# A gated attention and expert kernel: expert outputs scattered to token rows, slot clears in small transfers, first tiles' rows loaded ahead

## The reference

```
x = x + tanh(g_xattn) * layernorm(residual_scale * (attention(layernorm(x), context, mask) @ Wo + bo))   # 16 heads of 16
y = layernorm(x)
logits = y @ w_router                      # 8 experts
top 2 of 8; softmax of the two             # weights of a token
h = relu(y @ w_fc[e])^2 ; out = h @ w_proj[e]      # for the two experts e of the token
x = x + tanh(g_ffn) * sum of the two outputs, weighted
```

## Time and profile before

| | |
|---|---|
| median of 3 executions | 1218.92 us (1215.73 to 1224.65) |
| the profiled execution: its own time | 1217.37 us |
| its span, first to last instruction | 1215.6 us |
| TensorE busy / weight loads | 1130.4 us (93%) / 1081.4 us (89%) |
| VectorE busy | 864.5 us (71%) |
| ScalarE busy | 660.6 us (54%) |
| GpSimd busy | 131.1 us (11%) |
| mean granted TensorE clock | 0.978 of full speed |

### The profile page before, as it was taken

One profiled execution on the slowest core, in us unless ns is written; L12 is line 12 of the kernel. 1 busy time (PEld: TensorE's weight loads), 2 busy tenths in 40 slices (PEclk: granted clock), 3 DMA queues, 4 the chain that ended last, 5 costly groups with the idle time before them and its releaser, 6 DMA issues.

```text
span 1215.6 us, 55794 instructions
## 1 busy us (share of the span) xinstructions
PE 1130.4 (93%) x24824; PEld 1081.4 (89%) x24824; DVE 864.5 (71%) x2001; ACT 660.6 (54%) x838; POOL 131.1 (11%) x144
## 2 busy tenths in 40 slices
PE   6899999999999999999999999999999999878891
PEld 6899899999999999999999999999999999867790
DVE  5667677777777677767777777767777767747766
ACT  4456565656565556656565656555565655443430
POOL 0000000010101001010101010100101010100036
PEclk9899999999999999999999999999999999989896
DMA  5132222213231323232321313132322232024214
GB/s 179 57 88 72 83 69 69 85 54 104 67 92 55 104 68 104 68 87 68 87 82 47 109 64 100 49 103 67 104 68 87 64 99 67 17 61 124 82 61 138
DMA packets 59486, 98.83 MB, mean 81 GB/s; under 512 B 13109, under 2 KB 41586, under 8 KB 59250
## 3 DMA queue, kind: packets, MB, share of 16 engines
q1 hardware_dynamic: 49730, 79.93, 21.7%
q10 hardware_dynamic: 6832, 8.92, 2.2%
q0 software_dynamic: 2688, 6.43, 1.7%
HBM read 70.17 MB, written 24.15 MB: 78 GB/s over the span
## 4 chain that ended last, share of the span: by engine, by line
PE 79%; DVE 10%; issue 4%; POOL 2%; DMA 2%; SPq 1%; ACT 1%; POOLq 0%; ACTq 0%; DVEq 0%
PE v_ps L563 21%; PE k_ps L566 20%; PE sc_ps L589 18%; PE o_ps L604 11%; DVE prob L1233 3%; POOL expert_out L488 2%; DVE kl L1014 2%; DVE vst L1029 1%; PE k_ps L621 1%; PE k_ps L628 1%; DVE c_lo L1020 1%; PE sc_ps L506 1%; DVE q_hi L1066 1%; PE sc_ps L507 1%; PE sc_ps L508 1%
## 5 line engine op out<-in xcount | busy, mean ns | idle before, releaser
L858 ACT ACTIVATE prob<-sc_ps,m_bias 125x896 f32<-125x896 f32 x384 | 377.1, 1008 | 354.1 <-PE sc_ps L589 353.6
L563 PE MATMUL v_ps<-wv_hi,c_hi 64*125 64x256 f32 x1520 | 311.9, 285 | 2.9 <-DVE c_lo L1020 2.6
L566 PE MATMUL k_ps<-c_hi,wk_hi 64*128 64x500 f32 x760 | 306.8, 404 | 0.0
L563 PE MATMUL v_ps<-wv_lo,c_hi 64*125 64x256 f32 x1520 | 302.1, 279 | 0.0
L563 PE MATMUL v_ps<-wv_hi,c_lo 64*125 64x256 f32 x1520 | 302.0, 278 | 0.0
L566 PE MATMUL k_ps<-c_lo,wk_hi 64*128 64x500 f32 x760 | 294.0, 387 | 0.0
L566 PE MATMUL k_ps<-c_hi,wk_lo 64*128 64x500 f32 x760 | 293.2, 386 | 0.0
L1029 DVE TENSOR_TENSOR vst<-v_ps,rowv 125x512 f32<-125x512 f32 x191 | 131.3, 687 | 185.4 <-PE v_ps L563 185.4
L1233 DVE TENSOR_SCALAR prob<-prob 125x896 f32<-125x896 f32 x384 | 233.1, 620 | 39.8 <-ACT prob L858 39.8
L589 PE MATMUL sc_ps<-q_lo,kh 64*125 64x224 f32 x1536 | 233.3, 272 | 12.9 <-issue 12.9
L563 PEld LDWEIGHTS v_ps<-wv_hi,c_hi 64*125 64x125 f32 x1520 | 226.8, 184 | 17.0 <-issue 5.9
(11 more groups left out here) (189 smaller groups left out, 1639.6 us busy)
## 6 DMA issues: line engine op xcount, KB each, us to landing
raw<-in_ctxT SPq DMA_DIRECT2D x96, 500.0 KB, 3.5
slot_rows<-zero_row SPq DMA_DIRECT2D x16, 896.0 KB, 8.8
w_raw<-in_we ACTq DMA_DIRECT2D x16, 256.0 KB, 8.0
rows<-slot_rows SPq DMA_DIRECT2D x32, 128.0 KB, 2.0
slot_out<-y SPq DMA_DIRECT2D x32, 128.0 KB, 1.9
rec<-inv_scratch SPq DMA_DIRECT2D x64, 56.0 KB, 2.0
xq<-in_x ACTq DMA_DIRECT2D x16, 112.0 KB, 3.7
xr<-in_x ACTq DMA_DIRECT2D x16, 112.0 KB, 4.5
```

Source lines behind the costliest of these rows:

```text
L563: v_last = pe.matmul(v_ps[0:TC, j * D:(j + 1) * D], c_s[v_rows, cs], w_m[v_rows, k, :], start=begin and j == 0, stop=end, skip_group_check ...
L566: k_last = pe.matmul(k_ps[:, half, 0:TG], w[k_rows, k, ws], c_m[k_rows, :], start=begin, stop=end)
L858: act.activation(prob[0:TC, c % PB, :].rearrange("p (c n) -> p c n", c=2), sc_ps[0:TC, 2 * (c % 2):2 * (c % 2) + 2, 0:NH * S // 2], ACT.Ex ...
```

## The change

- `slot_rows` gets 8 more columns (rows of 1056 bytes). Column 256 holds, as an integer, the row of a new DRAM tensor `expert_rows` (2 x 14 x 112 rows) to which the expert's output for this slot belongs: one row for each token and each of its two experts. Cleared rows carry a number past the end.
- `clear_slots(i, e)` clears 128 rows of one expert. There are 14 x 8 of them, one or two behind the load of each group; each waits until the one before it has landed. The very first waits for `dest_done`, set by VectorE in its preamble once the numbers are in place.
- `send(j, r)`: the first send of a pair (r = 0) stays where it was; VectorE then rewrites the number (`relabel`, u = 9), and the second (r = 1) goes out after `inv_std(2)`.
- Each tile's output is scattered to `expert_rows` by GpSimd (`send_back`) as soon as it is out of PSUM; numbers past the end are dropped. SP's stores and `rows_back` are gone.
- After the last scatter SP loads `expert_rows` in eight plain DMAs. Of each chunk of pairs VectorE combines all but the last pair; ScalarE scales and GpSimd adds that one. `out` is stored in five parts.
- The rows of the first tiles are loaded once k and v are computed and the sends have landed (seven tiles), and the others once the exponentials are done; `turn(0)` stands ahead of the last attention products.
- The table work is split over u = 7, 9 and 10 of the last pair, and the steps of `beside_experts` are moved.

The diff, cut to its core (declarations, and removed lines that the listing above shows, are left out):

```diff
+RR = 12
+RE = 7
+WR = D + 8
+SPARE = 2 * NS * PW
+CB = ((0, 4), (4, 8), (8, 12), (12, 14))
...
+            return {0: 0, 2: 3, 4: 6, 7: 12, 8: 14, 9: 15, 11: 18, 12: 20, 14: 23, 15: 24, 17: 26, 18: 28}[at]
...
+            def clear_slots(i, e):
+                if i == 0 and e == 0:
+                    sp.wait_ge(dest_done, 2)
+                wait(sp, zeroed, 16 * (i * NE + e))
+                sp.dma_start(slot_rows[e * CAP + i * P:e * CAP + (i + 1) * P, :], zero_row[:, :]).then_inc(zeroed, 16)
             def pair(i):
                 for q in range(PG):
...
                         gather_sums(i - 1)
                     if i > 0 or q >= 2:
                         load_group(i * PG + q, q % 2)
-                    if q == 2:
-                        clear_slots(i)
+                    if i < CAP // P:
+                        for e in ((0, 1), (2,), (3,), (4,), (5,), (6, 7))[q]:
+                            clear_slots(i, e)
                     if q == 4 and i > 0:
                         spread_inverses(i - 1)
                 if i > 0:
...
             def load_slots(u):
                 if u == 0:
                     sp.wait_ge(tab_done, 2)
-                    sp.wait_ge(zeroed, 16 * NP)
+                    sp.wait_ge(zeroed, 16 * NE * (CAP // P))
                     for r in range(2):
                         sp.wait_ge(sent[r], 16 * NS)
-                    sp.wait_ge(pv_done, B * NC)
-                wait(sp, turned, u - RR + 1)
+                    sp.wait_ge(kproj_done, KD * NP * PG)
+                    sp.wait_ge(vproj_done, 2 * NP * PG)
+                if u == RE:
+                    sp.wait_ge(exp_done, B * NC)
+                if u >= RR:
+                    sp.wait_ge(turned, u - RR + 1)
+                    sp.wait_ge(back[u % NB], 16 * ((u - RR) // NB + 1))
                 row = sp.value_load(tab[0:1, 1, u:u + 1], min_val=0, max_val=NE * CAP - SL)
...
+                sp.dma_start(rows[:, u % RR, :], slot_rows[bass.ds(row, SL), :]).then_inc(rows_in[u % RR], 16)
+            def load_outputs(b):
+                j0, j1 = CB[b]
+                for r in range(2):
+                    at = r * NS * PW
+                    sp.dma_start(expert_out[0:PW, r, j0:j1, :],
+                                 expert_rows[at + j0 * PW:at + j1 * PW, :].rearrange("(j p) d -> p j d", p=PW))\
+                        .then_inc(expert_in[b][r], 16)
             for u in range(RR):
                 load_slots(u)
             gather_sums(NP - 1)
             spread_inverses(NP - 1)
...
+            for u in range(RR, NU):
+                load_slots(u)
+                if u == RR + 3:
                     pack(NP - 1)
...
+            for u in range(NU - NB, NU):
+                sp.wait_ge(back[u % NB], 16 * (u // NB + 1))
+            for b in range(len(CB)):
+                load_outputs(b)
+            sp.wait_ge(acc_done, 2 * NE)
+            sp.dma_start(out[:, NS:NP, :], acc[0:PW, NS:NP, :]).then_inc(out_done, 16)
+            for b, (j0, j1) in enumerate(CB):
+                sp.wait_ge(sum_done[0], 2 * (j1 - 1 - b))
+                sp.wait_ge(sum_done[1], 2 * (b + 1))
+                sp.dma_start(out[:, j0:j1, :], acc[0:PW, j0:j1, :]).then_inc(out_done, 16)
+            sp.wait_ge(out_done, 16 * (len(CB) + 1))
...
+            def send(j, r):
+                if r == 0:
+                    pool.wait_ge(slot_done, j + 1)
+                    pool.wait_ge(zeroed, 16 * NE * min(j + 1, CAP // P))
+                else:
+                    pool.wait_ge(relabelled, j + 1)
+                wait(pool, sent[r], 16 * j)
+                pool.indirect_dma_start(slot_rows[:, :], bass.IndirectOffsetOnAxis(ap=slot_i[0:PW, j, r:r + 1], axis=0),
+                                        y_row[0:PW, j % 2, :], None).then_inc(sent[r], 16)
...
+                    send(j, 0)
                 if not first:
                     inv_std(2, i - 1)
+                for j in ranked(i):
+                    send(j, 1)
...
+            def send_back(u):
+                pool.wait_ge(y2_evac, u + 1)
+                wait(pool, back[u % NB], 16 * (u // NB))
+                pool.indirect_dma_start(expert_rows[:, :],
+                                        bass.IndirectOffsetOnAxis(ap=rows[:, u % RR, D:D + 1].bitcast(i32), axis=0),
+                                        y2[:, u % NB, :], None, bounds_check=SPARE - 1, oob_is_err=False)\
+                    .then_inc(back[u % NB], 16)
+            for u in range(NU):
+                send_back(u)
+                if u == 11:
+                    x_plus_beta(NP - 1)
+                    inv_std(1, NP - 1)
+                if u == 13:
+                    inv_std(2, NP - 1)
+            for b, (j0, j1) in enumerate(CB):
                 for r in range(2):
...
+                    pool.wait_ge(scaled, 2 * b + r + 1)
+                    wait(pool, sum_done[1], 2 * b + r)
+                    pool.tensor_tensor(acc[0:PW, j1 - 1, :], acc[0:PW, j1 - 1, :], expert_out[0:PW, r, j1 - 1, :], ALU.add)\
+                        .then_inc(sum_done[1], 1)
...
+            turn(0)
             for d in range(GC, 0, -1):
                 pv(NP - 1, PC - d)
-            turn(0)
...
+            act.wait_ge(weights_done, 1)
+            for b, (j0, j1) in enumerate(CB):
+                for r, weight in enumerate((pr1, pr2)):
+                    act.wait_ge(expert_in[b][r], 16)
+                    act.activation(expert_out[0:PW, r, j1 - 1, :], expert_out[0:PW, r, j1 - 1, :], ACT.Copy,
+                                   scale=weight[0:PW, j1 - 1:j1]).then_inc(scaled, 1)
...
+                if i < NS:
+                    dve.tensor_copy(label(i), dest_i[0:PW, i, 0:1])
+                normalised(2, i, y_row[:, i % 2, 0:D], acc[:, i, :]).then_inc(y_done, 1)
+            def label(i):
+                return y_row[0:PW, i % 2, D:D + 1].bitcast(i32)
+            def relabel(i):
+                for j in ranked(i):
+                    dve.wait_ge(sent[0], 16 * (j + 1))
+                    dve.tensor_copy(label(j), dest_i[0:PW, j, 1:2]).then_inc(relabelled, 1)
...
+                if u == 9 and final:
+                    tile_starts()
+                if u == 10 and final:
                     tile_table()
-                if u == 8 and final:
-                    rows_back()
+                if u == 9:
+                    relabel(i)
...
+            dve.wait_ge(ones_done, 5)
+            dve.tensor_copy(zero_row[:, D:D + 1].bitcast(i32), spare_c).then_inc(dest_done, 1)
+            dve.tensor_copy(dest_i[:, :, :], dest_c.rearrange("p (j r) -> p j r", r=2)).then_inc(dest_done, 1)
...
-                    wait(dve, y2_out[u % NB], 16 * (u // NB))
-                    dve.tensor_copy(y2[:, u % NB, :, :], sc_ps[:, 2 + u % 2, 0:SH * D].rearrange("p (h d) -> p h d", h=SH))\
-                        .then_inc(y2_evac, 1)
+                    wait(dve, back[u % NB], 16 * (u // NB))
+                    dve.tensor_copy(y2[:, u % NB, :], sc_ps[:, 2 + u % 2, 0:D]).then_inc(y2_evac, 1)
...
+            for b, (j0, j1) in enumerate(CB):
+                for r, weight in enumerate((pr1, pr2)):
+                    dve.wait_ge(expert_in[b][r], 16)
+                    if r == 1:
+                        dve.wait_ge(sum_done[0], 2 * (j0 - b) + j1 - 1 - j0)
+                    for j in range(j0, j1 - 1):
+                        dve.scalar_tensor_tensor(acc[0:PW, j, :], expert_out[0:PW, r, j, :], weight[0:PW, j:j + 1],
+                                                 acc[0:PW, j, :], ALU.mult, ALU.add).then_inc(sum_done[0], 1)
...
+    expert_rows = nc.dram_tensor("expert_rows", (SPARE, D), mybir.dt.float32, kind="Internal").ap()
```

More of the change, by code:

```diff
@@ L48 @@
 FILL = 10
[L51 removed]
+CST = (P, NE, HS, KD, KD, PW, NE, NE * NE, CAP // SL, NU, 1, 2 * NS)
 EPS = 1e-5
@@ L115, in gated_cross_attention_moe @@
         cst = sb("cst", [P, sum(CST)])
-        ident, rev_e, hmask, bk, bq, below_c, seg_c, upto_c, size_c, step_c = (cst[:, sum(CST[:i]):sum(CST[:i + 1])] for i in range(len(CST)))
+        ident, rev_e, hmask, bk, bq, below_c, seg_c, upto_c, size_c, step_c, spare_c, dest_c = (cst[:, sum(CST[:i]):sum(CST[:i + 1])] for i in range(len(CST)))
         rowv = sb("rowv", [P, 4 * D + 3])
@@ L435, in _ @@
             pool.memset(ones[:, :], 1.0).then_inc(ones_done, 1)
-            pool.wait_ge(ones_done, 4)
+            pool.memset(y_row[:, :, :], 0.0).then_inc(ones_done, 1)
+            pool.wait_ge(ones_done, 5)
             def inv_std(ln, i):
@@ L452, in expert_lo @@
                                    plain(we_hi[:, bass.ds(i, 1), :, :].squeeze(1)), ALU.subtract).then_inc(welo_done, 1)
-            def send(j):
-                pool.wait_ge(slot_done, j + 1)
-                pool.wait_ge(zeroed, 16 * (j + 1))
-                for r in range(2):
-                    wait(pool, sent[r], 16 * j)
-                    pool.indirect_dma_start(slot_rows[:, :], bass.IndirectOffsetOnAxis(ap=slot_i[0:PW, j, r:r + 1], axis=0),
```

(13 more changed lines are left out.)

98 lines of the change are left out of this document (20 added, 78 removed).

## The result

The changed kernel took 1269.06 us (median of 4 runs, 1266.10 to 1274.27) where the kernel before took 1219.6 on the same chip: a ratio of 1.0408, 95% interval 1.0356 to 1.0459. The sign was forecast; the size was not (1240, range 1210 to 1260). The profiled execution spans 1264.3 us, 48.7 more than before.

A forecast was written before the change was run, and what follows sets the result against it. TensorE, 79% of the chain, was taken to bound the kernel in the first 1070 us. Terms -16.5+7+36+12-6-1-10 = +21.5 on 1217.37 gave 1238.9, about 1240 for the median, range 1210 to 1260.

The forecast's parts named there:

- clears, the gaps: TensorE's 15 gaps, one per pair, 16.7 us in all, vanish with the 896 KB clears: -16.5 us.
- start: Three small clears ahead of context group 2's load delay the first exponential from 23.49 to 29.8: +7 us.
- second send: Pairs 3 to 14: y_rows waits for the later send, landing in 4.8 us; y transpose 3.0 us late: +36 us.
- clock: Behind that wait TensorE's clock drops, costing 1.7 us in 60% of twelve pairs: +12 us.
- last pair, experts: Split table work and earlier first expert rows give -6 us; scatters hidden in the expert stage and pack earlier give -1.
- tail: After the static experts, eight loads replace the gathers and VectorE does 20 multiply-adds instead of 28: -10 us.
- Rival 3: Worse contention at the second send: landing 6.0 us and a clock drop in all twelve pairs, 1263 us; chance 0.10.
- rival 4: Splitting the clears fails: fetches are delayed by anything queued, the 15 gaps stay, +16.5, 1256 us; chance 0.10.
- Rivals 1 and 2: Second send lands in 3.8 us, clock never falls, 1216 (chance 0.20); or lands in 2.5 us, 1200 (chance 0.13).

## Why the prediction was wrong

By its own steps, on the first kind of chip:

| step | predicted | measured | from |
|---|---|---|---|
| clears, the gaps | -16.5 | -21 | B 33.92 to 32.53, 15 times |
| start | +7 | +7.4 | first exponential |
| second send | +36 | +50.6 | A summed over 12 pairs, less 12 x 3.76 |
| clock | +12 | +25 | B over 32.53 (ten pairs, 20.4), the next two stretches over those with three buffers (4.8) |
| last pair, experts | -7 | -3 | +62.4 at the last pair's y transpose, +59.4 at the combine |
| tail | -10 | -10.7 | +59.4 to +48.7 |
| sum | +21.5 | +48 | span +48.7 |

The rows leave some 3 us between the first and the fifth term open: the split table work saved about 3 us ahead of the last pair's y transpose as well, which would make the clears some -19 and the fifth term some -5. The sum stays.

**The step that failed is the size of "The second send", the landing time of 4.8 us.** Its mechanism, place and count were right: buffer, parity, pairs 3 to 14, no slack at the y transpose. I took 4.8 as the mean of the first sends, which start beside a load (they took 4.0 to 6.0; my 3.8 for the fastest was a little low). The second send starts beside the same load and has w_raw and xr about it as well. I named these two and gave them no price. In the changed kernel the twelve landed in 5.4 to 7.2 us but for the control at 3.6, 6.3 in the mean, so even my upper bound of 6.0 was below most of them. The first sends, which now have small clears about them, took longer too, 5.6 in the mean. The two runs that took raw and then w_raw out of its way show what each was worth.

**The second failing size is the clock.** I took a drop of 3.4 us, as after the idle time in the earlier trace rows, in 60% of the pairs. The idle time was 4.5 us, the lower level lasted 6.8 us in nine pairs and 3.4 in two, about 5 of it behind the wait, and eleven of twelve pairs had it: 2 to 2.5 us for the 1.0 that I took in the mean. The two errors hang together: a landing 1.5 us later costs as much more wait, and the runs with waits of 4.5, 1.8 and 0.8 us had the drop in eleven, ten and none of twelve pairs. I had judged an idle time of 2.9 us to "lie at the edge" and taken a mean there; the load held back shows that already 1.8 us mostly brings the drop, so it was no edge, and the range should have held both sides in full. Rival 3, given 0.10, came nearest: 1263 from a landing of 6.0 and a drop in all twelve.

**What held.** The gaps went with the 896 KB transfers, so rival 4 fell; the small clears alone showed it in the kernel before. Rivals 1 and 2 fell with the landing time. The start was right to 0.4 us and was shown by undoing it. The tail was right: the 20 multiply-adds took 10.16 us for the 9.3 taken; that is read from the two profiles, and no run undid it. Of the last pair I had the order of events but somewhat too much gain: its y transpose now waits 3.24 us (0.30 before). That this and the two second sends in a row account for the rest is my reading; no run undid them either.

The Trainium skill's formula for such a send (DMA: Bandwidth & Descriptors, the anatomy of one DMA on the GpSimd path), 2.3 us here by my estimate, comes near the fastest of the 28 sends, 2.6, and is far below those that went beside loads (3.6 to 7.2).

## What to carry to other kernels

Before a send or a load is moved later, find the step that refills its buffer, and count buffers until that step waits for a transfer of the round before: here one more buffer turned +4.1% into -2.2%. Price a transfer by the company it will have at its new place, every queue counted, not by its median at the old one. An idle time of TensorE costs its own length and a slower stretch behind it, which only the granted clock shows. And a ratio near one can be two large effects that cancel on one chip and not on the next.

## What was not expected of the hardware

- One program on two kinds of chips: 1216.5 and 1260 us (once 1235.25 on a chip of the second kind), with the same A and B, and the difference only where instructions of TensorE came late beside DMAs of GpSimd (25 products in 28 us beside the gathers; C 11.6 instead of 10.4 us beside two sends and a load). What makes the kinds differ is open.
- A 112-row send of some 118 KB landed in 2.6 us alone and in up to 7.2 beside 868 KB of loads on other queues.
- Filling an idle time with products restored the clock and hardly the time.
- The clock fell behind an idle time of 1.81 us in the run with the load held, and not behind one of 1.82 in the same run, nor behind the 2.15 of the earlier trace rows; it never fell behind the 0.7 to 1.2 us of the run with load and matrix moved, but did so once behind 0.77 us (0.63 us of idle time just ahead of it) in the changed kernel on the second kind of chip. The idle time's length alone did not decide it. The 13 us behind that 0.77:

```profile
920.50:933.50 13.00, 12.91 (x261) 12.55 (x263) 7.89 (x17) 6.81 (x9) 0.00 (x0) 0.87 0.28 80
```
